# The first normalisation moved inside the block of the first attention

## The reference

```python
x = x + tanh(g_xattn[0]) * L0_xattn(layernorm(x), ctx, ctx, mask, ...)   # 16 heads of 16
x = x + tanh(g_ffn[0])   * L0_ffn(layernorm(x), ...)                     # 8 experts, top 2, capacity
x = x + tanh(g_xattn[1]) * L1_xattn(layernorm(x), ctx, ctx, ...)         # 16 heads of 64, own norm, gamma, beta
x = x + tanh(g_ffn[1])   * L1_ffn(layernorm(x), ...)                     # 8 experts, top 2
```

## Time and profile before

| | us |
|---|---|
| median of 3 runs | 1609.89 (1609.64 to 1610.91) |
| the profiled execution's own time | 1613.79 |
| its span | 1612.0 |
| PE busy in the span | 1314.5 (82%) |
| DVE, ACT, POOL busy | 879.0, 800.7, 410.6 |

### The profile page before, as it was taken

One profiled execution on the slowest core, in us unless ns is written; L12 is line 12 of the kernel. 1 busy time (PEld: TensorE's weight loads), 2 busy tenths in 40 slices (PEclk: granted clock), 3 DMA queues, 4 the chain that ended last, 5 costly groups with the idle time before them and its releaser, 6 DMA issues. The chain is left out here.

```text
span 1612.0 us, 36347 instructions
## 1 busy us (share of the span) xinstructions
PE 1314.5 (82%) x10688; PEld 1042.5 (65%) x10689; DVE 879.0 (55%) x2927; ACT 800.7 (50%) x2195; POOL 410.6 (25%) x711
## 2 busy tenths in 40 slices
PE   2799999998199998049999999999999998369960
PEld 2566666666188888037777777778787876246640
DVE  3466676666244544536666666666676767122223
ACT  3577777777154543135555555555564656023320
POOL 2335554454301010720011212121212111300016
PEclk9899999999599999569999999999999999679985
DMA  5912222210233420220000000000000015112213
GB/s 122 416 64 88 90 88 84 87 50 19 79 131 144 156 104 26 73 93 11 11 12 11 22 11 22 11 22 11 22 10 22 1 37 222 61 37 64 65 58 108
DMA packets 47373, 111.35 MB, mean 69 GB/s; under 512 B 10828, under 2 KB 31500, under 8 KB 43468
## 3 DMA queue, kind: packets, MB, share of 16 engines
q1 hardware_dynamic: 37188, 96.25, 17.0%
q0 software_dynamic: 8192, 13.15, 2.9%
q10 hardware_dynamic: 1872, 0.68, 0.3%
HBM read 70.37 MB, written 43.84 MB: 71 GB/s over the span
## 5 line engine op out<-in xcount | busy, mean ns | idle before, releaser
L759 ACT ACTIVATE b_prob<-b_prob,b_low 100x361 f32<-100x361 f32 x256 | 154.9, 605 | 99.9 <-DVE b_low L871 99.9
L608 PE MATMUL b_ps_p<-b_context_part,b_wk_part 128*128 128x362 f32 x768 | 158.2, 343 | 0.0
L767 ACT COPY b_prob_t<-b_ps_t 128x300 f32<-128x300 f32 x256 | 103.5, 404 | 104.9 <-PE b_ps_t L672 102.4
L1414 ACT ACTIVATE a_prob<-a_prob,a_low 100x361 f32<-100x361 f32 x256 | 153.3, 601 | 4.4 <-DVE a_low L1548 4.4
L614 PE MATMUL b_ps_p<-b_wv_part,b_context_part 128*128 128x512 f32 (+1 forms) x576 | 151.4, 405 | 0.0
L871 DVE CUSTOM_DVE_ANT_0 b_prob<-b_ps_s,b_mask_bias 100x361 f32<-100x361 f32 x256 | 121.2, 530 | 36.7 <-PE b_ps_s L662 21.4
L1548 DVE CUSTOM_DVE_ANT_0 a_prob<-a_ps_s,a_mask_bias 100x361 f32<-100x361 f32 x256 | 121.4, 531 | 35.1 <-PE a_ps_s L1315 31.8
L672 PE MATMUL b_ps_t<-ident,b_prob 100*128 100x100 f32 x768 | 119.0, 264 | 24.6 <-ACT b_prob_t L767 24.1
L1422 ACT COPY a_prob_t<-a_ps_t 128x300 f32<-128x300 f32 x256 | 97.5, 407 | 82.7 <-PE a_ps_t L1325 81.5
L608 PEld LDWEIGHTS b_ps_p<-b_context_part,b_wk_part 128*128 128x128 f32 x768 | 125.2, 190 | 0.2 <-issue 0.2
L672 PEld LDWEIGHTS b_ps_t<-ident,b_prob 100*128 100x128 f32 x768 | 79.0, 143 | 69.4 <-issue 53.1
(11 more groups left out here) (295 smaller groups left out, 2634.6 us busy)
## 6 DMA issues: line engine op xcount, KB each, us to landing
rows_in<-zero SPq DMA_DIRECT2D x44, 512.0 KB, 4.9
w<-in_c_fc SPq DMA_DIRECT2D x8, 1024.0 KB, 6.1
w<-in_c_proj SPq DMA_DIRECT2D x8, 1024.0 KB, 4.9
a_context<-in_ctx SPq DMA_DIRECT2D x16, 361.0 KB, 3.5
b_context<-in_ctx SPq DMA_DIRECT2D x16, 361.0 KB
rows_in<-rows_in SPq DMA_DIRECT2D x8, 512.0 KB, 4.1
f_xe<-rows_in SPq DMA_DIRECT2D x8, 512.0 KB, 3.3
rows_out<-f_ye SPq DMA_DIRECT2D x8, 512.0 KB, 2.6
```

The lines of the kernel that those rows point to most:

```text
L608: ins = nc.tensor.matmul(bank[:, 0:LN2], w_parts["k"][a][:, k, t * P:(t + 1) * P], cx_parts[s][b][:, k, :], start=m == 0, stop=m == DK * l ...
L759: nc.scalar.activation(prob[0:S, k, 0:L], prob[0:S, k, 0:L], ACT.Exp, bias=low[0:S, k:k + 1], scale=-1.0, accum_out=total[0:S, k:k + 1]).t ...
L1414: nc.scalar.activation(prob[0:S, k, 0:L], prob[0:S, k, 0:L], ACT.Exp, bias=low[0:S, k:k + 1], scale=-1.0, accum_out=total[0:S, r:r + 1]).t ...
```

## The change

Block two and block three are gone. Their instructions stand in the attention's block, quarter by quarter. The two contexts and masks, and all that SP issues behind them, are issued when that block begins. On PE, the transposes of quarters 0 and 1 come first, then the first two projections of `pre`, the transposes of quarter 2, the next two projections, the transposes of quarter 3, and the value projections. ACT and DVE have a matching order. The banks for the transposes are now the six of the scores and of the transposed probabilities, so quarter 3 uses those of quarter 0 again. POOL's conversion of the first mask comes after its memsets. The tanh and the products with gamma and beta come last ahead of the first pair. The semaphores of `Norm` are made once for both of its uses, with the second counting on from the first.

```diff
--- before.py
+++ after.py
@@ -1058,6 +1058,9 @@
     pre = Units(layer, [("Q", 0, 0, 0), ("K", 0, 0, 0), ("Q", 0, 1, 0), ("K", 0, 1, 0)]
                 + [("V", 0, t, 0) for t in range(KT_N)])
     n_units, n_pre = len(full.units), len(pre.units)
+    pre_at = list(enumerate(pre.units))
+    norm = Norm(nc, T, "n0_", ctx, ps_s + ps_t, T["norm"], 0)
+    quarter_in = [nc.alloc_semaphore(f"{nm}quarter_in{k}") for k in range(DK)]
     router = Router(nc, T, 0, sb)
     T["dispatched"].append(router.dispatched)
     T["summed"].append(router.summed)
@@ -1214,12 +1217,12 @@
             router.credit_pool(pool)
             lo_ready.credit(pool)
             half_lower.credit(pool)
-            convert(0, 1, None)
             for part in (k_hi, k_lo):
                 pool.memset(part[:, :, L:LN2].bitcast(F32), 0.0).then_inc(zeroed, 1)
             pool.memset(prob[:, :, L:KT_N * P], 0.0).then_inc(zeroed, 1)
             for s in range(2):
                 pool.memset(vt[s][:, :, :], 0.0).then_inc(zeroed, 1)
+            convert(0, 1, None)
             for u, unit in enumerate(pre.units):
                 if unit[0] in ("Q", "K"):
                     lower(unit, pre.split[u], 0, True)
@@ -1375,9 +1378,28 @@
 
             for k in (scored, turned, valued, unit_done):
                 k.credit(pe)
+            def turn_quarter(q):
+                if q == Norm.GROUPS - 1:
+                    for k in range(DK):
+                        pe.wait_ge(quarter_in[k], 1)
+                norm.turn(pe, q, q + 1)
+
+            pe.wait_ge(T["ident_ready"], 1)
+            turn_quarter(0)
+            turn_quarter(1)
             pe.wait_ge(T["weights_in"][0], T["weights_in_value"][0])
-            for u, unit in enumerate(pre.units):
+            for k in range(DK):
+                pe.wait_ge(quarter_in[k], 1)
+            for u, unit in pre_at[:2]:
                 project(u, unit, pre, 0)
+            turn_quarter(2)
+            for u, unit in pre_at[2:4]:
+                project(u, unit, pre, 0)
+            turn_quarter(3)
+            for u, unit in pre_at[4:]:
+                project(u, unit, pre, 0)
+            for k in range(DK):
+                pe.wait_ge(quarter_in[k], Norm.GROUPS)
             pe.wait_ge(zeroed, 5)
             pe.wait_ge(taken.sem, taken.before(n_pre))
             pe.wait_ge(lo_ready.sem, lo_ready.before(pre.splits))
@@ -1450,7 +1472,26 @@
             for k in (exped, pt_ready, hi_ready):
                 k.credit(act)
             router.credit_scalar(act)
-            take(list(enumerate(pre.units)), pre, 0)
+
+            def centre(q):
+                norm.roots(act, q, q)
+                norm.apply(act, q, q, T["x"], T["xn"])
+
+            def keep_quarter(q):
+                norm.keep(act, nc.scalar.copy, q, 0).then_inc(quarter_in[0], 1)
+
+            centre(0)
+            centre(1)
+            keep_quarter(0)
+            centre(2)
+            keep_quarter(1)
+            take(pre_at[:2], pre, 0)
+            centre(3)
+            keep_quarter(2)
+            take(pre_at[2:4], pre, 0)
+            keep_quarter(3)
+            act.wait_ge(T["small_in"], 16 * 13)
+            nc.scalar.activation(T["gate"][:, :], T["gate_in"][:, :], ACT.Tanh).then_inc(T["built_gate"], 1)
             iterations(act, steps)
 
         @block.vector
@@ -1601,7 +1642,30 @@
             for k in (maxed, inverted, widened, kept_out, out_ready, taken, whole_ready):
                 k.credit(dve)
             router.credit_vector(dve)
-            take(list(enumerate(pre.units)), pre, 0)
+
+            def measure(q):
+                dve.wait_ge(T["x_in"][q // 2], 16)
+                norm.moments(dve, q, T["x"])
+                norm.scales(dve, q, q, 1.0, LN_EPS, 0.0)
+
+            def keep_quarter(q):
+                norm.keep(dve, nc.vector.tensor_copy, q, 1).then_inc(quarter_in[1], 1)
+
+            measure(0)
+            measure(1)
+            keep_quarter(0)
+            measure(2)
+            keep_quarter(1)
+            dve.wait_ge(T["small_in"], 16 * 13)
+            dve.wait_ge(T["consts"], 17)
+            take(pre_at[:2], pre, 0)
+            measure(3)
+            keep_quarter(2)
+            take(pre_at[2:], pre, 0)
+            keep_quarter(3)
+            dve.wait_ge(T["built_gate"], 1)
+            for k in ("gamma", "beta"):
+                nc.vector.tensor_scalar(T[k][:, :], T[k][:, :], T["gate"][:, 2:3], None, ALU.mult)
             iterations(dve, steps)
 
     ctx.close()
...
...
@@ -1667,54 +1731,18 @@
     def turn(self, pe, q, nth):
 
         nc, T = self.nc, self.T
-        pe.wait_ge(self.normed, nth)
+        pe.wait_ge(self.normed, self.first + nth)
         for k in range(DK):
             for j in range(self.PER):
                 c = (q * self.PER + j) * D + k * P
-                ins = nc.tensor.transpose(self.banks[q * DK + k][:, j * S:(j + 1) * S], T["xn"][0:S, c:c + P],
+                ins = nc.tensor.transpose(self.banks[(q * DK + k) % len(self.banks)][:, j * S:(j + 1) * S], T["xn"][0:S, c:c + P],
                                           T["ident"][0:S, 0:S])
             ins.then_inc(self.turned, 1)
 
     def keep(self, eng, copy, q, k):
-        eng.wait_ge(self.turned, q * DK + k + 1)
+        eng.wait_ge(self.turned, (self.first + q) * DK + k + 1)
         w = self.PER * S
-        return copy(self.T["xn_t"][:, k, q * w:(q + 1) * w], self.banks[q * DK + k][:, 0:w])
-
-
-def normalise(nc, T, nm):
-
-
-    with ExitStack() as ctx:
-        banks = [ctx.enter_context(nc.psum_tensor(f"{nm}bank{k}", [P, 512], F32)) for k in range(8)]
-        norm = Norm(nc, T, nm, ctx, banks)
-        q_all = range(Norm.GROUPS)
-
-        with nc.Block() as block:
-
-            @block.vector
-            def _(dve):
-                for q in q_all:
-                    dve.wait_ge(T["x_in"][q // 2], 16)
-                    norm.moments(dve, q, T["x"])
-                    norm.scales(dve, q, q, 1.0, LN_EPS, 0.0)
-                    if q:
-                        norm.keep(dve, nc.vector.tensor_copy, q - 1, 1)
-                norm.keep(dve, nc.vector.tensor_copy, Norm.GROUPS - 1, 1)
-
-            @block.scalar
-            def _(act):
-                for q in q_all:
-                    norm.roots(act, q, q)
-                    norm.apply(act, q, q, T["x"], T["xn"])
-                    if q:
-                        norm.keep(act, nc.scalar.copy, q - 1, 0)
-                norm.keep(act, nc.scalar.copy, Norm.GROUPS - 1, 0)
-
-            @block.tensor
-            def _(pe):
-                pe.wait_ge(T["ident_ready"], 1)
-                for q in q_all:
-                    norm.turn(pe, q, q + 1)
+        return copy(self.T["xn_t"][:, k, q * w:(q + 1) * w], self.banks[(q * DK + k) % len(self.banks)][:, 0:w])
 
 
 def experts_first(nc, T, D_):
@@ -1782,7 +1810,7 @@
                 pool.indirect_dma_start(out=got[k][s][0:S, :], out_offset=None, in_=YS[:, :],
                                         in_offset=bass.IndirectOffsetOnAxis(ap=gath[0:S, k, b:b + 1], axis=0)).then_inc(gathered[s], 16)
 
-    norm = Norm(nc, T, nm, ctx, ps)
+    norm = Norm(nc, T, nm, ctx, ps, T["norm"], 1)
 
     def combine(dve):
         for b in range(B):
@@ -2403,12 +2431,16 @@
     T["run"], T["have"], T["firsts"] = sb("run", [P, 2, 2, E]), sb("have", [P, E]), sb("firsts", [P, E], I32)
     T["exponents"] = sb("exponents", [P, len(EXPONENTS), 2])
     T["unique"], T["offset"] = sb("unique", [P, 2, 2]), sb("offset", [P, 2, 2])
+    T["norm"] = Norm.signals(nc)
     gate_in, T["gate"] = sb("gate_in", [P, 4]), sb("gate", [P, 4])
+    T["gate_in"] = gate_in
     T["x_in"] = [nc.alloc_semaphore(f"x_in{q}") for q in range(2)]
     T["ident_ready"] = nc.alloc_semaphore("ident_ready")
     T["weights_in"] = [nc.alloc_semaphore(f"weights_in{n}") for n in (0, 1)]
     T["w_in"] = [nc.alloc_semaphore(f"expert_in{s}") for s in range(2)]
-    small_in, consts, built, built_gate = (nc.alloc_semaphore(k) for k in ("small_in", "consts", "built", "built_gate"))
+    for k in ("small_in", "consts", "built_gate"):
+        T[k] = nc.alloc_semaphore(k)
+    small_in, consts = T["small_in"], T["consts"]
     zero_ready = nc.alloc_semaphore("zero_ready")
     D_["cleared"], D_["cleared_value"] = [nc.alloc_semaphore(f"cleared{n}") for n in (0, 1)], (16 * 2 * E, 16 * CLEARS)
     w_first = [(f"w{k}0", f"w{k}0") for k in "qkv"]
@@ -2505,24 +2537,6 @@
             pool.wait_ge(consts, 16)
             nc.gpsimd.tensor_scalar(T["offset"][:, 1, :], T["offset"][:, 1, :], float(E * Router.STRIDE), None,
                                     ALU.add).then_inc(consts, 1)
-
-    normalise(nc, T, "n0_")
-
-    with nc.Block() as block:
-
-        @block.scalar
-        def _(act):
-            act.wait_ge(small_in, 16 * 13)
-            nc.scalar.activation(T["gate"][:, :], gate_in[:, :], ACT.Tanh).then_inc(built_gate, 1)
-
-        @block.vector
-        def _(dve):
-            dve.wait_ge(small_in, 16 * 13)
```

(26 more changed lines are left out.)

## The result

The changed kernel takes 1589.28 us (median of 4 runs, 1585.11 to 1593.18) against 1610.4 us (4 runs, 1609.64 to 1612.98) for the kernel before, run beside it: a ratio of 0.9866, 95% interval 0.9838 to 0.9893. The gain is 21.1 us. The direction was right; 5.7 us of gain were missed.

What follows compares the result with a forecast made beforehand. Two chains, compute and DMA, were taken to bound the first iteration, with DMA setting or tying the third context's point at 63.2 against 78.59. That 15.4 us off the median 1609.89 gave 1594.5 us, range 1590.5 to 1599.5.

Steps and rivals of the forecast that it cites:

- The DMA chain: SP's load queue: first context issued about 11.7 instead of 31.93; gain 14.0 to 16.6 us, middle 15.3.
- the DMA again sets this point, or ties with compute: PE's start on the third context: at 61.9 to 64.5, middle 63.2, against 78.59; 15.4 us gained.
- a wait of more than 1.52 us: Sign: PE waits for the third context longer than the 1.52 us of before, if the clock is full.
- The compute chain: Early path from statistics through projections to first scores: scores at 38.2 instead of 49.63, 11.4 us gained.
- I take 0 here: DVE's wait for thirteen small loads before query 0: lateness taken as 0, bounds 0 and 3.9 us.
- the late bound of 26.4: Latest landing of the small loads, if 5.4 us of new traffic came on top of 21; 3.9 us late.
- Loads past 25: Sign that the forecast is wrong: the small loads ahead of DVE's query 0 land past 25.
- rival A: Early path bounds: small loads or mask about 4 us late, third context at 67.8, gain 10.8, 1599.1 us; chance 0.20.
- the forecast's 15.4: Total gain in us, taken at PE's start on the third context: 63.2 against 78.59.
- After it the work is the same up to the end, in the same loops, at a clock of 1.00: Everything behind the third context's point: no further gain or loss up to the end.
- unchanged within 2 us: Sign: distance from the third context's projection, at 78.59 before, to the span's end stays the same within 2 us.
- the range: Forecast time of the whole kernel: 1590.5 to 1599.5 us, around 1594.5.

Runs made afterwards that it cites:

- The delayed issue: Changed kernel with SP issuing late weights, clears and expert weights only after PE's early projections, contexts still early: 1607.52 us, ratio 0.9986.
- the second profile: The changed kernel run and profiled again, no edit: 1590.14 us, ratio 0.9879.
- the padded: Changed kernel with eight already satisfied waits on each of five engines at the start of the attention's block: 1634.16 us, ratio 0.9921.
- the two-block profiles: Changed kernel with two empty blocks put back ahead of the attention, in two comparisons: ratios 0.9914 and 0.9941.
- the merged kernel: Kernel before with the gates' block merged into the attention's, in two comparisons: 1657.4 us, ratio 1.0067, and 1663.46 us, ratio 1.0089.

## Where the prediction was right, and where it failed

**The DMA chain: its times right, its place as the bound wrong.** Issue at 11.27, clears in by 50.1, third mask by 61.3: 15.7 and 17.3 us earlier, where the sum had 14.0 to 16.6. The delayed issue shows that none of the first pair's gain comes without it. But "the DMA again sets this point, or ties with compute" came out only as a near tie: PE did not wait for the third context at all, where the text wanted a wait of more than 1.52 us. Compute set the point, at 66.47 and 62.84.

**The compute chain: one term mis-sized.** "I take 0 here" for the small loads: they were in at 26.64, just past the late bound of 26.4, and passing it cost 3.3 us at once. The first scores gained 8.1, not 11.4. Loads past 25 were among the signs that the text had said would show it wrong, and this is the condition of rival A: A's point for the third context was 67.8, and the first profile has 66.47, a gain of 12.1 there. In the second profile, with one half-clock stretch less, it is 62.84, a gain of 15.8. Behind that point PE was at 2.4 GHz: from it to the second pair take 13.75 us in both profiles of the changed kernel, against 15.2 to 16.2 in the three of before, which the sum had not counted. So the first pair's mean gain, 15.5, is the forecast's 15.4 by luck: some 3 us less from the loads, 1.5 to 2 more from the clock behind the third context, and the half clock of the first profile ahead of it missing in the second.

**The failed step.** "After it the work is the same up to the end, in the same loops, at a clock of 1.00", with a distance to the end "unchanged within 2 us". The term was put at nothing, and the rest was 5.9 us shorter; this is what carries the time out of the range. The instructions are the same. But "at a clock of 1.00" rested on the one stretch from 100 to 146 us in the earlier trace rows, while the clock line of the earlier trace rows has a 5 at 400 to 440 us, 5 and 6 at 640 to 720, and 6 and 7 at 1370 to 1450, where the changed kernel's has 6 and 8. Half clock fills 226.3, 226.5 and 219.3 us of the rest in the three profiles of before, 213.1 and 216.7 in the two of the changed kernel. Where the 5.9 us lie: the start of the second experts, and the turns of the second attention. At the former, before:

```profile
1419.50 0.66 PE L2248 MATMUL f_ps<-ident,f_xe 128*128 128x128 f32 x2 [20.38 <-DMA f_xe<-rows_in]
1420.71 3.77 PE L2256 MATMUL f_ps<-w,f_xt 128*128 x4 [0.55 <-ACT f_xt L2313]
...
1426.39 3.78 PE L2256 MATMUL f_ps<-w,f_xt 128*128 x4 [1.48 <-ACT f_xt L2313]
```

and after:

```profile
1401.12 0.66 PE L2276 MATMUL f_ps<-ident,f_xe 128*128 128x128 f32 x2 [19.98 <-DMA f_xe<-rows_in]
1402.33 3.58 PE L2284 MATMUL f_ps<-w,f_xt 128*128 x4 [0.55 <-ACT f_xt L2341]
...
1407.81 1.98 PE L2284 MATMUL f_ps<-w,f_xt 128*128 x4 [1.69 <-ACT f_xt L2341]
```

The second group still runs at half clock before (3.78 us) and at full clock after (1.98). The half-clock stretch over this place is 44.4 us in before, 4 of 4, and 37.5 us in all 11 profiles with 16 packets; the 300 matmuls from number 9900 on, which hold most of it, take 96.5 us (mean of before's four profiles, 95.6 to 98.3) against 93.5 (mean of the eleven, 90.1 to 96.6). That is about 3 us. The six turns give about 2 us together (493.7 in the mean of before's four profiles, 491.9 in that of the changed kernel's three). The rest lies within what single executions differ by.

What is shown and what not: that padding and empty blocks, which compute nothing, give a part of the gain back behind the first pair, and that the number of fetched instruction packets changes with it, is shown. That the fetched code costs the time, and that its place decides, is argued only: what joins them is that they occur together. Which engine's code it is, why the kernel before, the padded and one of the two-block profiles have 44.4 us of half clock at the second experts (the other 41.0, the merged kernel 37.5), and why the merged kernel's turns are the longest (rests of 1555.6 and 1569.7 against 1547.3) is open. The range was too narrow for a second reason: single executions of one kernel have first pairs 2 to 4 us apart.

## What to carry to other kernels

When a prologue is moved up, work out two chains, compute and the load queue, and expect their later one; then ask which tiny load stands in the wake of the traffic just moved ahead. Give loads wanted at different times semaphores of their own, and issue what nobody wants yet behind what somebody does, the two together: the first alone gave nothing here, and the second alone was not run. And do not trust "the rest is the same": here it moved by 6 us in 1600, 0.4%, with the same instructions, and eight idle waits per engine moved it back by about as much. So give such a rest a bound of that size in a forecast, and keep a few such paddings as a control when a gain of this size is to be explained.

## What I had not expected of the hardware

Instruction packets are fetched in every turn of the second attention's loop, 5 or 10 per 82 us turn, and idle waits ahead of the loop change which. A 0.5 KB load took 13.0 us beside the first weights and 16.3 us beside a full queue. And the kernel before takes 1609 to 1611 us in some comparisons and 1646 to 1647 in others: 1000 to 3750 matmuls into the program take 252 us in its own first profile and 279 us there, with the same instructions. In the slower one PE stops for 2.3 us in turn after turn of the first attention's loop (at 200.4, 249.1, 297.2 and 345.2 us), with 3.4 to 6.8 us of half clock behind each stop; the first profile has no such stop there, and one stretch of half clock of 3.4 us in those turns. Why is open.
